# One step of the edge loop holds 256 edges instead of 128: two products per bank, one addition and one stored row

## The reference

```python
h_src = (x @ W_src).reshape(n, HEADS, OUT_DIM)          # 4 heads x 64
e = a_src[src] + a_dst[dst]
e = jnp.where(e > 0, e, NEG_SLOPE * e)
m = jax.ops.segment_max(e, dst, num_segments=n)
p = jnp.exp(e - m[dst])
denom = jax.ops.segment_sum(p, dst, num_segments=n)
alpha = p / jnp.maximum(denom[dst], 1e-16)
msg = alpha[:, :, None] * h_src[src]
out = jax.ops.segment_sum(msg, dst, num_segments=n).reshape(n, HC) + bias
```

## Time and profile before

| | us |
|---|---|
| median of 3 runs (4583.89 to 4587.39) | 4585.84 |
| span of the profiled execution | 5008.5 |
| time of the profiled execution beside its span | not given |
| projections, until the first turn | 448 |
| the 50 full turns | 2652 |
| the last two turns | 68 |
| expert stage | 1840 |

### The profile page before, as it was taken

How to read it: one execution, slowest core, us unless ns; L and a number is a source line. 1 busy time by engine, 2 the same in 40 slices (tenths; PEclk the granted TensorE clock), 3 DMA queues, 4 the chain that set the end, 5 groups by cost and what they waited for, 6 DMA issues and landing times. The chain is left out here.

```text
span 5008.5 us, 85791 instructions
## 1 busy us (share of the span) xinstructions
PE 4317.8 (86%) x23103; PEld 3414.7 (68%) x23104; DVE 3827.5 (76%) x9797; ACT 2279.7 (46%) x4346; POOL 1838.8 (37%) x1702
## 2 busy tenths in 40 slices
PE   8973888878888788878877887599999999999999
PEld 7852655555556556555555565388888888888888
DVE  8864777777777777777777787678778877887786
ACT  5531333333333333333333333366666666666666
POOL 2136666666666666666666664000000000000000
PEclk9986899988999898988898898799999999999999
DMA  5544666665666666666665665300000000000000
GB/s 183 172 137 124 176 179 182 193 177 172 179 181 194 179 179 178 175 179 189 179 173 171 178 186 169 110 22 26 26 26 13 26 26 22 17 26 26 19 20 17
DMA packets 440044, 601.74 MB, mean 120 GB/s; under 512 B 41544, under 2 KB 366672, under 8 KB 439888
## 3 DMA queue, kind: packets, MB, share of 16 engines
q1 hardware_dynamic: 360016, 378.46, 23.4%
q0 software_dynamic: 79872, 221.62, 17.5%
HBM read 312.66 MB, written 287.25 MB: 120 GB/s over the span
## 5 line engine op out<-in xcount | busy, mean ns | idle before, releaser
L855 POOL DMA_INDIRECT acc<-h_tab,strips x1664 | 1775.8, 1067 | 1013.5 <-issue 498.6
L989 DVE SCALAR_TENSOR_TENSOR acc<-acc,strips,ps 128x260 f32<-128x260 f32 x1664 | 793.8, 477 | 480.3 <-PE ps L1360 220.8
L1360 PE MATMUL ps<-acc 128*128 128x260 f32 x3328 | 1068.5, 450 | 44.4 <-DVE acc L989 27.3
L1360 PEld LDWEIGHTS ps<-acc 128*128 128x128 f32 x3328 | 647.5, 216 | 157.8 <-DVE acc L989 45.8
L974 DVE TENSOR_TENSOR acc<-acc 128x512 f32<-128x512 f32 x832 | 562.5, 681 | 0.0
L1863 ACT ACTIVATE exp<-ps,bn 128x512 f32<-128x512 f32 (+1 forms) x400 | 310.0, 775 | 492.4 <-PE ps L1930 489.0
L1177 ACT ACTIVATE strips<-ps 128x512 bf16<-128x512 bf16 x416 | 248.0, 596 | 553.9 <-remote 251.5
L1928 PE MATMUL ps<-w_hi,b_hi 128*128 128x256 f32 x1568 | 444.8, 284 | 1.2 <-DVE exp L1767 1.2
L1930 PE MATMUL ps<-w_hi,b_lo 128*128 128x256 f32 x1568 | 443.7, 283 | 0.0
L1929 PE MATMUL ps<-w_lo,b_hi 128*128 128x256 f32 x1568 | 443.6, 283 | 0.0
L1775 DVE TENSOR_TENSOR a_lo<-exp,a_hi 128x512 fp32r<-128x512 f32 (+1 forms) x400 | 261.1, 680 | 169.8 <-ACT a_hi L1865 146.2
(11 more groups left out here) (264 smaller groups left out, 8485.5 us busy)
## 6 DMA issues: line engine op xcount, KB each, us to landing
side_tab<-acc SPq DMA_DIRECT2D x416, 520.0 KB
acc<-h_tab,strips POOLq DMA_INDIRECT x1664
acc<-xnt_tab SPq DMA_DIRECT2D x50, 512.0 KB
h_tab<-proj SPq DMA_DIRECT2D x25, 520.0 KB, 6.6
exp<-side_tab SPq DMA_DIRECT2D x100, 130.0 KB, 2.3
proj<-in_x SPq DMA_DIRECT2D x25, 512.0 KB, 5.3
base_tab<-proj SPq DMA_DIRECT2D x25, 512.0 KB, 3.2
xnt_tab<-proj SPq DMA_DIRECT2D x25, 512.0 KB, 6.0
```

Source lines behind the costliest of these rows:

```text
L855: pool.indirect_dma_start(G[s][:, b * GU + u], None, h_tab, bass.IndirectOffsetOnAxis(REC[s][:, b * GU + u, 0:1], 0)).then_inc(g_in[s], 16)
L989: nc.vector.scalar_tensor_tensor(A[:, (b % 2) * GU + u], A[:, (k - 1) % (2 * GU) if k else 2 * GU], smt[s][:, k:k + 1], ps[u][:, 0:MW], AL ...
L1360: nc.tensor.matmul(ps[u][:, 0:MW], S32[b % 2][:, u], G[s][:, b * GU + u], start=True, stop=True).then_inc(g_mm.sem, 1)
```

## The change

A step now holds two edge tiles (DU = 2, 256 edges) of one node tile. A group keeps its 32 edge tiles, and so its 32 gathers, 16 message multiplies, 8 one-hots and 32 products, but has 16 steps (NS), two a block (BS). The two products of a step accumulate in one bank, one addition follows, and one row per step is stored. Steps go round the four banks (k % 4). There are now 782 edge pairs and up to 98 node boundaries: 880 steps, 55 groups. The tables of the steps shrink accordingly; `fetch` reads four blocks' numbers at once, twice a turn. The written-out end of the rings becomes seven groups long (REST), of which the last three have no mix work.

```diff
+DU = 2
+BS = GU // DU
+NS = GS // DU
...
-    TE = -(-E // P)
-    NG = -(-(TE + NT - 1) // GS)
+    TE = -(-E // (DU * P))
+    NR = N // P + 1
+    NG = -(-(TE + NR) // NS)
     NB = NG * GQ
-    STEPS = NG * GS
+    STEPS = NG * NS
...
-        msg_set, g_mm, acc_add = stage("msg_set", 2 * GQ), stage("g_mm", GS), stage("acc_add", GS)
+        msg_set, g_mm, acc_add = stage("msg_set", NS), stage("g_mm", NS), stage("acc_add", NS)
...
+        REST = NG - 2 * (NCH - 1)
+        assert REST >= AHEAD
+        FETCH = GQ // 2
...
-            ring(eng, NG, 2, body, ahead=AHEAD, hint=hint)
+            ring(eng, NG, 2, body, ahead=REST, hint=hint)
...
-                nc.vector.tensor_copy(t_step[:, seg], ps[7][64:65, 0:SW])
-                nc.vector.tensor_copy(t_num[:, seg], ps[7][0:GS, 0:SW])
+                nc.vector.tensor_scalar(t_step[:, seg], ps[7][64:65, 0:SW], float(DU), None, ALU.mult)
+                for u in range(DU):
+                    nc.vector.tensor_scalar(t_parts[:, seg, u], ps[7][0:GS, 0:SW], float(DU), float(u), ALU.mult, ALU.add)
...
                     for b in range(GQ):
-                        acc_add.wait(sp, g, GU * (b + 1))
+                        acc_add.wait(sp, g, BS * (b + 1))
                         pass_on(sp, "sp")
                         k, v = b % 2, at(side_v, g * GQ + b)
-                        sp.dma_start(v, A[:, k * GU:(k + 1) * GU]).then_inc(side_out[k], 16)
+                        sp.dma_start(v, A[:, k * BS:(k + 1) * BS]).then_inc(side_out[k], 16)
...
-                        g_mm.wait(pool, g - 2, GU * (b + 1))
+                        g_mm.wait(pool, g - 2, BS * (b + 1))
...
-                def add(g, s, b, u):
-
-                    k = b * GU + u
+                def add(g, s, b, i):
+
+                    k = b * BS + i
                     g_mm.wait(dve, g, k + 1)
...
-                    nc.vector.scalar_tensor_tensor(A[:, (b % 2) * GU + u], A[:, (k - 1) % (2 * GU) if k else 2 * GU],
-                                                   smt[s][:, k:k + 1], ps[u][:, 0:MW], ALU.mult, ALU.add
+                    nc.vector.scalar_tensor_tensor(A[:, k % (2 * BS)], A[:, (k - 1) % (2 * BS) if k else 2 * BS],
+                                                   smt[s][:, k:k + 1], ps[k % 4][:, 0:MW], ALU.mult, ALU.add
                                                    ).then_inc(acc_add.sem, 1)
...
                             add(g, s, b, 0)
                             if b < GQ - 1:
                                 message(g, s, b + 1, 1)
-                            add(g, s, b, 1)
...
                             mix_between(n, s * GQ + b)
-                            add(g, s, b, 2)
...
-                            add(g, s, b, 3)
+                            add(g, s, b, 1)
...
                 def aggregate(g, s, b, i):
-                    msg_set.wait(pe, g, 2 * b + i + 1)
+                    k = b * BS + i
+                    msg_set.wait(pe, g, k + 1)
                     if i == 0:
                         s_ev.wait(pe, g, b + 1)
-                    for u in (2 * i, 2 * i + 1):
-                        if b:
-                            acc_add.wait(pe, g, (b - 1) * GU + u + 1)
-                        else:
-                            acc_add.wait(pe, g - 1, (GQ - 1) * GU + u + 1)
-                        nc.tensor.matmul(ps[u][:, 0:MW], S32[b % 2][:, u], G[s][:, b * GU + u], start=True, stop=True
-                                         ).then_inc(g_mm.sem, 1)
+                    if k >= 4:
+                        acc_add.wait(pe, g, k - 3)
+                    else:
+                        acc_add.wait(pe, g - 1, NS + k - 3)
+                    for u in range(DU):
+                        ins = nc.tensor.matmul(ps[k % 4][:, 0:MW], S32[b % 2][:, i * DU + u], G[s][:, b * GU + i * DU + u],
+                                               start=u == 0, stop=u == DU - 1)
+                    ins.then_inc(g_mm.sem, 1)
...
-                            if b in (0, 1, 3, 5):
+                            if b in (0, 3):
                                 fetch(b + 1 if b else 0)
```

More of the change, by code:

```diff
@@ L232, in build @@
         t_at = rt.at
-        t_num = rt.take(STEPS, parts=GS)
+        t_num = rt.take(STEPS * DU, parts=GS)
+        t_parts = t_num.rearrange("p (s u) -> p s u", u=DU)
         j_step = work_t[32:33, t_at:t_at + STEPS].bitcast(i32)
@@ L265, in build @@
         pick = r4.take(GS, parts=GS)
-        smt = [r4.take(GS) for _ in range(2)]
+        smt = [r4.take(NS) for _ in range(2)]
         adb = r4.take(NT * 3 * HEADS // 2, dt=bf16).rearrange("p (j q h) -> p j q h", q=3, h=HEADS)
@@ L324, in build @@
         rs_set, rs_mm, rs_exp, rs_done = stage("rs_set", 5), stage("rs_mm"), stage("rs_exp"), stage("rs_done")
-        msg_set, g_mm, acc_add = stage("msg_set", 2 * GQ), stage("g_mm", GS), stage("acc_add", GS)
+        msg_set, g_mm, acc_add = stage("msg_set", NS), stage("g_mm", NS), stage("acc_add", NS)
         bn_st = stage("bn_st", 2 * (RSQ + 2))
         edge_v = a["edge"].rearrange("t a p -> t (a p)")
-        side_v = side_tab.rearrange("(b u) p c -> b p u c", u=GU)
-        BOUND = "the tables hold edge tiles up to TE and node tiles below NT by their making"
+        side_v = side_tab.rearrange("(b u) p c -> b p u c", u=BS)
+        BOUND = "the tables hold edge tiles up to DU * TE and node tiles below NR by their making"
         LAST_BOUND = "the last step of a node tile lies below STEPS by its making"
         AHEAD = 3
+        REST = NG - 2 * (NCH - 1)
+        assert REST >= AHEAD
+        FETCH = GQ // 2
         def step_values(engine, table, b, most):
-            lo = b * GU
-            sl = table[:, lo:lo + 2 * GU] if isinstance(b, int) else table[:, bass.ds(lo, 2 * GU)]
+            lo = b * BS
+            sl = table[:, lo:lo + FETCH * BS] if isinstance(b, int) else table[:, bass.ds(lo, FETCH * BS)]
             return nc.values_load_multi_w_load_instructions(sl, engines=[engine], min_val=0, max_val=most,
@@ L343, in chunks @@
         def chunks(n):
-            return not (isinstance(n, int) and n >= NCH), not (isinstance(n, int) and n == 0)
+            return not (isinstance(n, int) and n >= NCH), not (isinstance(n, int) and not 0 < n <= NCH)
         def turns(eng, turn, hint):
@@ L799, in build @@
         G = [r3.take(GS, MW) for _ in range(2)]
-        A = r3.take(2 * GU + 1, MW)
+        A = r3.take(2 * BS + 1, MW)
         S32 = [r3.take(GU, P) for _ in range(2)]
@@ L1059, in mix_between @@
                         statistics(n - 1, 1, 1)
-                    if i == 10:
+                    if (cur or prev) and i == 10:
                         deviations(n)
@@ L1149, in same_steps @@
                     acc_add.wait(act, q - 2)
-                    lo = q * GS
-                    nc.scalar.activation(smt[sq], same[:, lo:lo + GS] if isinstance(q, int) else same[:, bass.ds(lo, GS)],
+                    lo = q * NS
+                    nc.scalar.activation(smt[sq], same[:, lo:lo + NS] if isinstance(q, int) else same[:, bass.ds(lo, NS)],
                                          ACT.Copy).then_inc(sm_cp.sem, 1)
@@ L1533, in fetch @@
                     def fetch(k):
-                        js = step_values(ET.PE, j_step, q * GQ + k, NT - 1)
-                        tiles_of[k], tiles_of[k + 1] = js[0:GU], js[GU:2 * GU]
+                        js = step_values(ET.PE, j_step, q * GQ + k, NR - 1)
+                        for i in range(FETCH):
+                            tiles_of[k + i] = js[i * BS:(i + 1) * BS]
                     def look(k):
@@ L2051 @@
     arrays["x"] = np.concatenate([g["x"], np.zeros((NP - N, D), np.float32)])
[L2052 to L2053 removed]
+    dst = np.concatenate([g["dst"], np.full(EP - E, N, np.int32), np.full(GS * P, -1, np.int32)])
+    src = np.concatenate([g["src"], np.zeros(EP - E + GS * P, np.int32)])
     arrays["edge"] = np.ascontiguousarray(np.stack([src.reshape(-1, P), dst.reshape(-1, P)], axis=1))
[L2055 removed]
+    ends = np.concatenate([dst[:EP].reshape(TE, DU * P)[:, -1], np.full(KC * P - TE, 1 << 20, np.int32)])
     arrays["last_dst"] = np.ascontiguousarray(ends.reshape(KC, P).T)
```

40 lines of the change are left out of this document (20 added, 20 removed).

## The result

The changed kernel takes 4661.56 us (median of 4 runs, 4658.77 to 4666.85) where the kernel before takes 4584.86 (4 runs, 4581.61 to 4587.39): ratio 1.0169, 95% interval 1.0155 to 1.0183, 76.7 us slower. The forecast was 4549, range 4445 to 4655. The time lies inside the first rival's 4634 to 4679.

The account below looks back on a forecast made before the run. Profiled turns were bound by hand-over between TensorE and VectorE, timed ones close to GpSimd's gathers. Full turns -130, three more groups +105, projections -12: -37, or 4549 us, range 4445 to 4655.

Parts of the forecast that it names:

- first rival: Gathers already set the timed turn: gain 0 to 0.9 us a turn, 4634 to 4679 us; chance 0.33, shared with TensorE.
- gather pace: Loop: least time GpSimd needs for a group's 32 gathers; 43.8 us profiled, taken as 42.6 in a timed run.
- the 422.7 us: Whole kernel: profiled span of 5008.5 over the median of 4585.84; 310 to 420 us laid mostly in the full turns.
- gain per turn: Full turns, timed: from 45.7 to 43.1 us, stopped at the gathers, 2.6 us each, -130 us over 50.
- timed turn of 45.7: Loop of the kernel before, without the profile: a full turn estimated at 44.7 to 46.8 us, taken as 45.7.
- Three more groups: End of the loop: 55 groups, each with 32 gathers; turn 50 to last addition 173 against 68 us, +105.
- Projections: Stage before the loop: smaller tables, 28 compares of about 0.22 us for 52 of 425 ns; -12, bounds -25 and 0.
- The expert stage: Last 1840 us of the span, TensorE busy 1780: left alone by the change, no gain or loss forecast.
- a turn of 48.3: Full turn of the profiled execution: 53.1 us less 4.8 for additions, bank depth and register loads; span 4860.
- The other two signs: Next profile: gathers that get longer, or a tail over 190 us, would show the prediction wrong.
- The factor of 0.6: Full turns: part of VectorE's 6.4 us saved on additions that somebody is waiting behind; 6.4 x 0.6 a turn.
- bank depth: Products in the loop: four banks hold two blocks, so TensorE's wait for additions goes; 0.5 us a turn, bounds 0 and 0.9.

## Why the prediction was wrong

**The failed step: the gather pace was taken too low.** "The gather pace in a timed run has bounds 40.0 and 43.8; I take 42.6" and half a microsecond. It measured 44.6, outside the bounds. The prediction gives no row for 42.6; what stands behind it is the idea that gathers are quicker when nothing records them, and that idea rests on the reading of the 422.7 us as recording. On the quick chip a gather is no shorter than on the slow ones (1.088 against 1.070 us in the earlier trace rows); it is the rest of the turn that is quicker. That VectorE's operations then meet the gathers more densely and make them the 0.018 us longer is argued, not tested. The gain per turn, forecast at 45.7 - 43.1 = 2.6, came out at an estimated 0.7: 50 x 1.9 = 95 us of the error of 112.6, as far as the estimate holds.

**Its root: a profile and a median of different chips.** The timed turn of 45.7 was right (an estimated 45.4), by luck: the difference of 422.7 us was rightly laid mostly into the full turns, for the wrong reason. What the prediction did say, that in the timed runs the loop runs close to GpSimd, is what happened; with 44.6 instead of 43.1 the same sum gives -55 + 105 - 12 = +38. The other 17 us of the error are the three terms that follow: +19, -18 and +16.

**Three more groups: +105 forecast, +124 measured.** 173 us from turn 50 to the last addition became 190.7, above the upper bound too. The forecast has the last gather issued 132 us after the start of turn 50, which is 96 gathers. It starts at 2764.4, 151.9 us after:

```profile
L867 POOL DMA_INDIRECT acc<-h_tab,strips x1760: 945/949/4007, 313.8 to 2764.4; - x196
```

GpSimd was behind when turn 50 began, with 108 gathers left and not 96, and they follow each other at 1.41 us and not at 43 / 32 = 1.34. From the last gather to the last addition it is 38.8 us, where the forecast had 5 + 18 + 18 = 41. So the whole of the excess lies in the gathers, and it is the same failed step once more.

**Projections: -12 forecast, -30 measured** on slow chips (448.5 to 418.0), outside the bounds of 0 and -25. The compares were to take 0.22 us. The shortest of L532 take 0.32, and most are held up:

```profile
L532 DVE TENSOR_SCALAR work<-work x28: 322/2462/2468, 33.7 to 296.0; 128x220 bf16<-128x220 f32 x28
```

```profile
44.80 2.49 POOL L794 TENSOR_TENSOR proj<-proj 128x1024 f32<-128x1024 f32 x1 [8.78 <-DVE proj L511]
44.97 2.46 DVE L532 TENSOR_SCALAR work<-work 128x220 bf16<-128x220 f32 x1
```

A compare that starts behind GpSimd's addition ends with it. 18 of 28 do, against 3 or 4 of 52 before. The stage gained 30 us all the same; which of its fewer operations gave them was not tried.

**The expert stage: nothing forecast, +16 measured.** "The change leaves the last part alone" is true of its work and not of its place in TensorE's instruction memory. The Trainium skill (Runtime: NRT & Kernel Launch, section Instruction fetch mechanics) says that code is fetched in blocks of 16 KiB, 256 instructions, that TensorE holds 128 KiB of it, and that a taken branch whose target is outside the window that is held forces a fetch before the engine goes on. The packets here are of that size (2.29 MB / 140). By these figures a loop of some 1690 instructions touches 7 or 8 blocks, by where it starts, and TensorE holds 8; that the eighth is one too many is not in the page but read from the runs, where one shift of three takes the packets from 140 to 51 and 17 to 20 us off the stage.

**Slow chips: a turn of 48.3 forecast from the old profile, 51.7 measured.** The profile that I read was of such a chip, so the step from 53.1 down to 48.3 can be checked among slow chips alone. "Wrong would make me: a profiled turn above 51 (VectorE was not the one waited for)": it is. The other two signs came as well, on the quick chip: gathers of 1.088 us, and a tail of 190.7. VectorE's busy time did fall by the forecast 6.4 us a turn (40.5 to 34.1), but it was not what the turn waited for. The factor of 0.6 on the 6.4 us of additions was mine. Additions, bank depth and stores together give 1.0 us a turn there, and cutting gathers gives 5.6 (before) and 7.3 (changed), though their reader does not wait for them. The trace shows stalls of up to 7.5 us in which TensorE, VectorE and ScalarE all rest and GpSimd goes on. One of the changed kernel on a slow chip, all engines:

```profile
2187.48 0.48 DVE L1001 SCALAR_TENSOR_TENSOR acc<-acc,strips,ps 128x260 f32<-128x260 f32 x1
...
2187.84 1.09 PE L1371 MATMUL ps<-acc 128*128 128x260 f32 x4
2188.21 0.37 SPq L851 DMA_DIRECT2D side_tab<-acc  x1
2188.53 0.95 POOL L867 DMA_INDIRECT acc<-h_tab,strips  x1 [0.30 <-issue]
2189.78 0.95 POOL L867 DMA_INDIRECT acc<-h_tab,strips  x1 [0.30 <-issue]
...
2191.03 0.94 POOL L867 DMA_INDIRECT acc<-h_tab,strips  x1 [0.30 <-issue]
2192.28 0.95 POOL L867 DMA_INDIRECT acc<-h_tab,strips  x1 [0.30 <-issue]
2193.54 0.94 POOL L867 DMA_INDIRECT acc<-h_tab,strips  x1 [0.30 <-issue]
2196.12 0.19 DVE L1012 TENSOR_SCALAR work<-ps 128x32 f32<-128x32 f32 x1 [8.16 <-remote]
2196.24 0.28 ACT L1207 ACTIVATE strips<-ps 128x128 f32<-128x128 f32 x1 [10.66 <-remote]
```

L1012 waits only for products that TensorE had finished before 2187. Counting the stretches of over 1.5 us in which TensorE, VectorE and ScalarE all rest, from turn 5 to turn 43 (some 2000 us): 22, 17 and 12 in the three profiles of before and 27 in the changed kernel on slow chips, 2 in the changed kernel on the quick one, 2 (before) and 0 (changed) with 24 gathers on a slow one, 27 and 38 with half the bytes and half the rows. So they go with the number of gather instructions. Over the 50 full turns they sum to 82, 59 and 45 us before and 124 us changed, that is 42 to 79 us more, where the change loses 50 x (2.7 - 1.0) = 85 us of its gain. But the changed kernel's 50 turns are some 350 us longer on the slow chip than on the quick one, and these stretches give 124 - 21 = 103 us of it; the rest lies in shorter waits. That they are late deliveries of what other engines had done is argued from these rows, not shown; why one chip is free of them is open.

**The rest.** The rival that came true is the first, by its own mechanism. Additions 880, products 3520 and register loads 110 were as forecast. GpSimd's real waits, forecast to fall from 496 to under 300 us, are 22.9 on the quick chip but still 443 on a slow one, the kind of chip that the 496 came from. "What is removed from VectorE does not speed them either" held: 1.070 to 1.074 us a gather on slow chips. The Trainium skill's rule (SBUF — State Buffer, section Who interferes with whom) was weighed only for the additions; the two experiments on the length of a gather agree with its other half, for with one SBUF input in the one-hots, then in the multiplies too, the gathers shorten by 3% and 9%. The section's inference that `tensor_tensor` leaves the making of descriptors alone, because it takes only the shared read interface, is not borne out where gathers lengthen beside such operations. The prediction's "one with a single SBUF input does not" left out the exception that the section makes, for VectorE's 2-port modes; the compares held up for 2.46 us have one SBUF input. Whether they run in such a mode, no run here shows.

## What to carry to other kernels

Count an engine's fixed gap between instructions as its work before calling it idle: GpSimd at 43% busy was the bound on the quick chip, and the test is whether anything but "issue" stands in its idle time. Check that the profile and the median are of the same machine before explaining the gap between them; a profiled execution timed beside others on its own chip would have shown that recording costs nothing. A change that trades cheap instructions on a waiting engine for more rounds of the bounding one can lose, as here, and even untouched code can move when the code ahead of it changes its length.

## What the runs showed of the hardware

- The same kernel takes 4585 us on one chip and 4986 to 5044 on five others, with much the same durations of single instructions (a gather 1.088 against 1.074 us, an addition 478 against 479 ns): the difference lies in the waits, and its cause is open.
- An indirect DMA takes GpSimd 0.95 + 0.30 us for 128 rows of 1040 bytes or of 520, and 0.90 + 0.30 for 64 rows: nearly all of it is per instruction.
- With no VectorE operation beside it a gather takes 0.95 us. Beside one of 1024 elements with two SBUF inputs (L1053) one took 1.66, and where several such operations follow each other they take up to 3.3 in the quick chip's full turns (VectorE and GpSimd):

```profile
1534.83 1.20 DVE L1053 TENSOR_TENSOR work<-work,rows 128x1024 f32<-128x1024 f32 x1
1535.18 1.66 POOL L867 DMA_INDIRECT acc<-h_tab,strips  x1 [0.30 <-issue]
...
1540.30 1.27 DVE L986 TENSOR_TENSOR acc<-acc 128x512 f32<-128x512 f32 x2
1540.92 3.22 POOL L867 DMA_INDIRECT acc<-h_tab,strips  x1 [0.30 <-issue]
1541.51 1.20 DVE L1059 TENSOR_TENSOR work<-work 128x1024 f32<-128x1024 f32 x1
1542.64 0.67 DVE L399 TENSOR_TENSOR strips<-iota_row,strips 128x512 bf16<-128x512 f32 x1
```

- A compare with one SBUF input (0.32 us alone) takes 2.46 us when it starts behind a GpSimd addition of 2.5 us.
- Shifting TensorE's code by 144 instructions is worth 17 to 20 us of 1860 in a stage that is otherwise the same.
